# Adding each state's product to the sum with a transfer of its own, in a selective scan between two feed-forward blocks

## The reference

```python
x = x + 0.5 * ffn(layernorm(x), w1, w2, w3)
x = x + attn(layernorm(x), W_x, W_dt, b_dt, A_log, D_param)
x = x + 0.5 * ffn(layernorm(x), w1, w2, w3)

def ffn(x, w1, w2, w3):          # q(w): clip(round(w / mean|w|), -1, 1)
    return (sigmoid(x @ q(w1).T) * (x @ q(w2).T)) @ q(w3).T      # 512 -> 1408 -> 512

def attn(x, ...):                # per token t, channel d, state n
    dt_raw, b, c = split(x @ W_x.T, [128, 16, 16])
    dt = softplus(dt_raw @ W_dt.T + b_dt)
    h = exp(dt * a) * h + dt * b * x       # a = -exp(A_log), a scan over the tokens
    y = sum over n of h * c
    return y + x * D_param
```

## Time and profile before

| | us |
|---|---|
| median of 3 runs | 840.51 |
| lowest, highest | 837.66, 843.51 |
| the profiled execution | 838.59 |
| its span, first to last instruction | 836.7 |
| mean granted PE clock, share of full | 0.894 |

### The profile page before, as it was taken

The page is one execution under the profiler, slowest core; times in us unless marked ns, Lnnn a source line. Parts: engine busy times, 40 slices in busy tenths (PEclk is TensorE's granted clock), DMA queues, the critical chain, the costliest instruction groups (busy, mean ns, idle before and its releaser), DMA issues.

```text
span 836.7 us, 13876 instructions
## 1 busy us (share of the span) xinstructions
PE 651.4 (78%) x4920; PEld 538.5 (64%) x4920; DVE 674.6 (81%) x1079; ACT 554.6 (66%) x1157; POOL 658.4 (79%) x516
## 2 busy tenths in 40 slices
PE   4688587368889888989899888988898876147578
PEld 4576375257677776777578767876687755136367
DVE  4962798699978997899978997899789978799721
ACT  5752764967696678776885679566966795366231
POOL 0261597799899989999899989998999898689112
PEclk7798797679999999999999998999999999569779
DMA  9400378677774978297829784878659673957300
GB/s 362 133 1 1 104 168 180 156 148 163 177 169 108 208 179 187 48 231 167 189 51 227 166 179 111 182 171 173 157 126 202 151 179 82 235 122 141 76 1 26
DMA packets 42694, 122.12 MB, mean 146 GB/s; under 512 B 5888, under 2 KB 14848, under 8 KB 42624
## 3 DMA queue, kind: packets, MB, share of 16 engines
q0 software_dynamic: 19152, 69.74, 44.5%
q1 hardware_dynamic: 23472, 51.49, 18.0%
HBM read 47.03 MB, written 4.46 MB: 62 GB/s over the span
## 4 chain that ended last, share of the span: by engine, by line
POOL 27%; DVE 20%; ACT 17%; PE 15%; issue 14%; DMA 7%; DVEq 0%; POOLq 0%; ACTq 0%
DVE states L881 11%; POOL shared L1078 11%; PE work L392 10%; DMA shared<-shared 7%; POOL hid_lo L1064 6%; PE stat L392 4%; DVE shared L893 3%; POOL shared L1090 3%; ACT decay L700 3%; POOL shared L1089 2%; POOL x_lo L1058 2%; POOL shared L282 1%; ACT tanh L643 1%; ACT hid_hi L651 1%; POOL square L286 1%
## 5 line engine op out<-in xcount | busy, mean ns | idle before, releaser
L1078 POOL TENSOR_TENSOR shared<-shared,b_row 128x1024 f32<-128x1024 f32 x128 | 331.2, 2658 | 39.8 <-DVE shared L282 21.8
L392 PE MATMUL work<-x_hi,q 128*128 128x256 f16 x1408 | 325.8, 281 | 45.8 <-DVE hid L856 25.8
L392 PE MATMUL work<-x_lo,q 128*128 128x256 f16 x1408 | 324.8, 280 | 0.0
L881 DVE TENSOR_TENSOR_SCAN states<-decay,last_state,shared 128x256 f32<-128x256 f32 x448 | 301.7, 738 | 4.9 <-DVE shared L893 0.5
L700 ACT ACTIVATE decay<-shared,a_neg 128x256 f32<-128x256 f32 x512 | 221.9, 468 | 95.6 <-DVE states L881 93.5
L1064 POOL TENSOR_TENSOR hid_lo<-hid,hid_hi 128x256 f16<-128x256 f32 x176 | 144.5, 1102 | 58.0 <-ACT hid_hi L651 57.9
L392 PEld LDWEIGHTS work<-x_hi,q 128*128 128x128 f16 x1408 | 142.5, 101 | 71.6 <-DVE hid L856 30.0
L392 PE MATMUL work<-hid_hi,q 128*128 128x256 f16 x704 | 165.9, 282 | 5.2 <-POOL hid_lo L1064 3.6
L392 PE MATMUL work<-hid_lo,q 128*128 128x256 f16 x704 | 165.9, 282 | 0.0
L893 DVE TENSOR_TENSOR shared<-states,c_row 128x1024 f32<-128x1024 f32 x128 | 156.0, 1219 | 9.5 <-DMA shared<-shared 2.2
L392 PEld LDWEIGHTS work<-x_lo,q 128*128 128x128 f16 x1408 | 141.7, 101 | 22.0 <-issue 1.1
(11 more groups left out here) (99 smaller groups left out, 733.1 us busy)
## 6 DMA issues: line engine op xcount, KB each, us to landing
shared<-shared POOLq DMA_DIRECT2D x133, 512.0 KB, 6.6
b_row<-bc_dram SPq DMA_DIRECT2D x32, 512.0 KB, 4.9
c_row<-bc_dram SPq DMA_DIRECT2D x32, 512.0 KB, 5.2
x_in<-xT SPq DMA_DIRECT2D x8, 512.0 KB, 5.4
outT<-shared SPq DMA_DIRECT2D x7, 512.0 KB, 4.5
shared<-w1T SPq DMA_DIRECT2D x4, 704.0 KB, 6.9
shared<-w2T SPq DMA_DIRECT2D x4, 704.0 KB, 11.8
shared<-w3T SPq DMA_DIRECT2D x3, 768.0 KB, 13.4
```

The lines of the kernel that those rows point to most:

```text
L392: return nc.tensor.matmul(out, lhsT, rhs, start=start, stop=stop)
L881: nc.vector.tensor_tensor_scan(out=states[:, k, :], data0=decay[pair][:, k % 2, :], data1=dbx[:, g % DBX_RING, k, :], initial=state, op0=A ...
L1078: nc.gpsimd.tensor_tensor(dbx[:, g % DBX_RING, :, :], u[:, par, :, :], bcast(b_row[:, group % 2, n % ROWS, :]), ALU.mult).then_inc(dbx_don ...
```

## The change

Each product gets a transfer of its own, issued in the state after it; even states still go to `x2`, odd ones to `y`, and each waits only for the one before it to the same sum. The ring has four single buffers, so a product waits for the transfer of the product four before. `add_y` waits for both last products. There are four semaphores (even and odd products, even and odd chunks) instead of two.

The tables have entries of their own for the first and the last chunk, and the middle order changes too. The softplus on ACT is cut into four pieces with places of their own, as is reading z and reading b and c. `ffn1_due` is general enough to place an entry of FFN 1 beyond a chunk's end; with these tables none lies there. In the middle chunks, on ACT the second identity and the logarithm move behind two gates, the high halves go later, `d_xln` and the high half of layer norm 0 now stand in front of the next chunk's first decays. On DVE the hidden blocks 3 and 4 of FFN 2 go behind the product of state 12, together with `centre` 0; on POOL the low halves 3 to 10 of FFN 2 come after `softplus[2]` and the fold of layer norm 0, and that norm's low half before the product of the next chunk's state 0. The order of PE stays, but for one or two hidden blocks of FFN 2 that move across z and mean 0. In the last chunk `add_y` moves from state 3 to state 1, `centre` 2 one state forward, hidden block 10 of FFN 2 from state 13 to 12, and both residuals into states 14 and 15; in the first, `hidden`, `residual` and the rest of FFN 1 move forward by up to a state, and the middle of layer norm 0 back.

```diff
-DBX_RING, PAIR_RING, X_RING, Y_RING = 3, 2, 3, 2
+DBX_RING, PROD_RING, X_RING, Y_RING = 3, 4, 3, 2
...
 AT_ACT = dict(
-    d_xln=152, dt_raw=101, gate1=[0, 2, 10, 11, 20, 21, 30, 32, 32, 32, 41],
-    gate2=[80, 90, 91, 92, 111, 120, 120, 122, 130, 131, 132], hi1=[2, 11, 20, 21, 22, 31, 32, 41, 41, 41, 42],
-    hi2=[100, 100, 100, 120, 130, 130, 130, 131, 140, 140, 140], logs=120, square0=121, square1=72, square2=50,
-    std0=140, std1=82, std2=60, x_hi0=150, x_hi2=62, z0=110, z1=120)
+    bc_read=101, bc_read_first=100, d_xln=142, d_xln_first=152, dt_raw=101, dt_raw_first=100,
+    gate1=[0, 2, 10, 12, 20, 22, 22, 32, 32, 41, 41], gate1_first=[0, 0, 2, 2, 2, 20, 20, 21, 22, 32, 40],
+    gate2=[72, 82, 91, 100, 112, 112, 120, 121, 131, 131, 132],
+    gate2_last=[80, 81, 91, 92, 92, 92, 101, 111, 111, 112, 121],
+    hi1=[12, 12, 22, 40, 40, 40, 40, 40, 41, 42, 42], hi1_first=[0, 2, 21, 21, 30, 30, 31, 40, 40, 40, 40],
+    hi2=[82, 100, 102, 122, 122, 131, 131, 140, 140, 140, 140],
+    hi2_last=[90, 92, 100, 101, 110, 111, 111, 111, 121, 122, 130], logs=[112, 112, 120, 120],
+    logs_first=[112, 121, 130, 130], square0=130, square0_first=130, square1=80, square1_first=72, square2=50,
+    square2_last=40, std0=140, std0_first=150, std1=90, std1_first=81, std2=60, std2_last=42, x_hi0=150,
+    x_hi0_first=150, x_hi2=61, x_hi2_last=70, z_read=[110, 110, 112, 112], z_read_first=[102, 102, 111, 111])
 AT_DVE = dict(
-    centre0=122, centre1=73, centre2=50, hid1=[2, 10, 12, 13, 22, 23, 32, 40, 42, 42, 43],
-    hid2=[90, 92, 93, 112, 120, 122, 122, 131, 133, 133, 140], norm0=142, norm1=92, norm2=63, recip0=140,
-    recip1=91, recip2=62, res1=[62, 71], res2=[153, 153])
+    centre0=130, centre0_first=132, centre1=73, centre1_first=72, centre2=50, centre2_last=33,
+    hid1=[2, 10, 12, 13, 22, 23, 32, 40, 42, 43, 43], hid1_first=[0, 2, 10, 11, 12, 20, 22, 30, 32, 33, 33],
+    hid2=[81, 83, 103, 123, 123, 130, 130, 131, 132, 140, 141],
+    hid2_last=[81, 90, 93, 93, 102, 103, 112, 113, 121, 122, 123], norm0=143, norm0_first=151, norm1=92,
+    norm1_first=91, norm2=70, norm2_last=62, recip0=141, recip0_first=151, recip1=91, recip1_first=83, recip2=62,
+    recip2_last=60, res1=[61, 71], res1_first=[60, 70], res2=[153, 153], res2_last=[150, 151])
 AT_POOL = dict(
-    add_y=30, fold_sq0=131, fold_sq2=50, lo1=[21, 30, 30, 30, 40, 40, 41, 42, 42, 42, 42],
-    lo2=[112, 112, 112, 131, 132, 132, 132, 132, 132, 132, 132], softplus=[131, 131, 132, 140], x_lo0=150,
-    x_lo2=70)
+    add_y=30, add_y_last=12, fold_sq0=131, fold_sq0_first=132, fold_sq2=50, fold_sq2_last=31,
+    lo1=[21, 22, 32, 42, 42, 42, 42, 42, 42, 42, 42], lo1_first=[20, 20, 30, 31, 31, 31, 31, 31, 31, 32, 32],
+    lo2=[102, 121, 122, 131, 131, 131, 131, 131, 131, 131, 131],
+    lo2_last=[92, 110, 110, 112, 122, 130, 130, 130, 130, 130, 130], softplus=[131, 131, 131, 132],
+    softplus_first=[132, 132, 140, 140], x_lo0=140, x_lo0_first=141, x_lo2=70, x_lo2_last=61)
+
+
+def at(table, c, name):
+    own = name + ("_first" if c == 0 else "_last" if c == NC - 1 else "")
+    return table[own] if own in table else table[name]
...
-            return 32 * (PAIRS * (c // 2) + n)
+        def added(c, n):
+
+            return (odd_added if n % 2 else even_added)[c % 2], 16 * (NS // 2 * (c // 2) + n // 2 + 1)
 
         def prod_of(c, n):
-            return prod[:, 2 * ((NS * c + n) // 2 % PAIR_RING) + n % 2, :, :]
+            return prod[:, (NS * c + n) % PROD_RING, :, :]
...
-                if g // 2 >= PAIR_RING:
-                    before = g // 2 - PAIR_RING
-                    dve.wait_ge(pair_added[before // PAIRS % 2], pairs_added(before // PAIRS, before % PAIRS + 1))
+                if g >= PROD_RING:
+                    dve.wait_ge(*added((g - PROD_RING) // NS, (g - PROD_RING) % NS))
...
-            def add_pair(c, pair):
-
-                if pair == 0:
+            def add_prod(c, n):
+
+                if n == 0:
                     pool.wait_ge(down_read, 2 * ffn1_pass(c) + 2)
+                elif n == 1:
                     pool.wait_ge(d_xln_done, c + 1)
                 else:
-                    pool.wait_ge(pair_added[c % 2], pairs_added(c, pair))
-                pool.wait_ge(prod_done, NS * c + 2 * pair + 2)
-                nc.gpsimd.dma_start(x2(c), prod_of(c, 2 * pair), accum_op=ALU.add).then_inc(pair_added[c % 2], 16)
-                nc.gpsimd.dma_start(y(c), prod_of(c, 2 * pair + 1), accum_op=ALU.add).then_inc(pair_added[c % 2], 16)
+                    pool.wait_ge(*added(c, n - 2))
+                pool.wait_ge(prod_done, NS * c + n + 1)
+                total = y(c) if n % 2 else x2(c)
+                nc.gpsimd.dma_start(total, prod_of(c, n), accum_op=ALU.add).then_inc(added(c, n)[0], 16)
...
                     if s == 0 and not first(c):
-                        add_pair(c - 1, PAIRS - 1)
-                    elif s > 0 and s % 2 == 0:
-                        add_pair(c, s // 2 - 1)
+                        add_prod(c - 1, NS - 1)
+                    elif s > 0 and not (last(c) and s == NS - 1):
+                        add_prod(c, s - 1)
```

194 lines of the change are left out of this document (99 added, 95 removed).

## The result

| | us |
|---|---|
| kernel before, median of 4 runs on the same chip | 839.09 (836.74 to 843.51) |
| changed kernel, median of 4 runs | 852.55 (848.63 to 855.06) |
| ratio, 95% interval | 1.0157 (1.0118 to 1.0196) |
| profiled execution of the changed kernel, its span | 848.63, 846.8 |

The changed kernel is 1.6% slower, where I predicted 1.5% faster. The profiled execution of the changed kernel is the fastest of its four, its span 10.1 us longer than that of before (836.7).

The account below looks back on a forecast made before the run. A middle chunk was taken as a VectorE part, then a ScalarE-then-TensorE part in series. Terms -2.2 -4.7 -3.2 -1.9 +0.5 +0.6 -0.9 -1.2 sum to -13.0 us, from 840.5 to 827.5; range 817 to 840 (own 821 to 832).

Parts of the forecast that it names:

- The low half ahead of the next chunk's first product: POOL, chunk's end: that product ends at about U+30.0 instead of +26.5, DVE wants it at +31.5; costed at nothing.
- y's transfer: Middle chunks: y lands earlier, so DVE's wait at the centring of layer norm 2 goes, -4.7 us over six chunks.
- Ring waits: DVE's waits for product buffers that a transfer hasn't freed go, -2.2 us.
- The last chunk: Earlier y cuts the centring wait (-3.2 us), the down projection wait before the residual goes (-1.9), last products wait (+0.5).
- The middle order, U to residual: Middle chunks, state 11's scans to second residual: square root and second down projection end as before, 0 us.
- The last middle chunk: It has no layer norm 0, so the high halves come sooner there, -0.9 us.
- before U: Middle chunks: gate and high half ahead of a square root cost a hidden-unit slot, +0.6 us over six chunks.
- First chunk: Split softplus lets decays in between, but other waits appear on DVE; -1.2 us (0 to -4).
- Slower: the eight low halves: Rival, chance 0.13: POOL's low halves wait for ACT's late square, delaying six chunks; up to +23 us, 850.
- The slow stretch goes: Rival, chance 0.15: PE's lower-clock stretch in the down projection goes, -10 us more, 817.
- The middle gives nothing: Rival, chance 0.25: middle and first chunks gain nothing; only the last chunk and the -0.9 before it remain, -7.4 us, 833.1.

Follow-up runs that it names:

- e5: Changed kernel with layer norm 0's low half on POOL back behind the next chunk's first product and its transfer: 837.0 us, ratio 0.9988 to the kernel before.
- e8: Kernel before with single transfers, the new first- and last-chunk orders and, in middle chunks, only POOL's order new: 834.2 us, ratio 0.9963.
- e9: As e8, but layer norm 0's low half back behind the next chunk's first product on POOL: 835.6 us, ratio 0.9949 to the kernel before.
- e11: As e5, but each product's transfer halved, leaving half of the products out of the sum: 830.7 us, ratio 0.9896 to the kernel before.
- e1: Kernel before with one transfer for each product and a ring of four, every order as before: 838.1 us, ratio 0.9985.
- e16: As e8, but the last chunk in its old order: 836.7 us, ratio 0.9966 to the kernel before.
- e18: As e5, but ACT's gate of FFN 2 unit 5 behind the logarithm: 835.5 us, ratio 0.9948 to the kernel before.
- e3: Changed kernel with middle chunks in the old order, keeping single transfers and the new first- and last-chunk orders: 838.2 us, ratio 0.9991.

## Why the prediction was wrong, step by step

**The low half ahead of the next chunk's first product: "costed at nothing with 1.5 us of cover left".** This step failed, and it made the kernel slower: with it undone (e5) the changed kernel is level with before, 0.9988. The 13 us that I had promised are missing there too, for the reasons further down. Its place was sized well: the product ends at U+30.7 (U is the end of the scans of state 11; predicted 30.0), and DVE does not wait for it. But I asked only who waits for the product. Behind it on POOL stand the transfers of products 13 to 15 and of the next chunk's first two, then y's, then FFN 1's low halves. In three of the five chunks the transfers moved 0.6 to 2.7 us against e5's, and e5 prices that at 15.6 us (14.2 by the ratios) where the sum has 0. I had also missed the 0.73 us wait for ACT's high half in front of it. Why the same place costs nothing beside the other engines' old orders (e8, e9) is argued above, not shown.

**y's transfer: -4.7.** The mechanism was read wrongly, and the wait that was to go (4.7 us) doubled, to 9.5. I took the landing of 6.6 us as what a transfer takes when one other is ahead, and "lands about 6.6 us after issue" came from counting those ahead. The median of all 133 is 6.6 before and 6.9 after, and from y's issue to the mean it takes 8 to 10 in the middle chunks of both kernels, in a stretch in which the engines' share is 0.97 and more. And not one but two transfers are still under way when y goes out, as before: the products' transfers ahead of it now go out some 3 to 4.6 us apart, and each takes 6 to 10 us there. y took 0.8 us less to land on the mean, not three. And it went out 2.1 us later, counted from U, where I had allowed 0.6; in e5, without the low half in front, it is 0.6. In e11, with half of the bytes, what I had promised is there: no centring wait in any middle chunk. The Trainium skill (DMA: Bandwidth & Descriptors, Anatomy of one DMA) gives 2.0 us and bytes over 436 GB/s. For 256 KB less that is 0.6 us, an estimate; here the medians fell by 2.3 us (6.9 to 4.6). All of the products' transfers were halved there, so a transfer also had fewer bytes of others beside it: the page's figure per transfer doesn't carry over to transfers that add, in a full queue.

**Ring waits: -2.2.** Right: gone in e1 and in the changed kernel. What I didn't price is the transfer that they put ahead of the low halves with the old middle order, 0.8 us a chunk in e1.

**The last chunk: -3.2 for the centring, -1.9 for the residual, +0.5.** The residual's wait is gone and the last sum waits 0.85, inside my 0 to 2. The centring's wait grew from 3.99 to 5.10, against 0.8 predicted. The chunk from product to product fell by 1.1 us, where my terms say 4.6. By e16 its own order is worth nothing that can be measured. What failed in the term of 3.2 is the time of y's issue, which I put at +8 from its place in POOL's order, though `add_y` waits for product 15: it went out at +11.6. Its landing took 6.2 us, about the 6.6 that I had put.

**The middle order, U to residual: 0.** The back part is 0.8 us longer in three of five chunks, 1.2 in one and 0.7 shorter in one; in the one PE's clock fell for longer, in the other not at all. The square root ends at +19.4 and not +18.7 in four of the five, because I laid ACT's gates out by their durations alone and not by when PE has their block ready (0.88 us in the trace; e18 bears it out in part). The low halves end at +22.3 in the same four, instead of +21.6. DVE's stall came out at 2.39 in four chunks, predicted about 3.

**The last middle chunk: -0.9, and before U: +0.6.** The first is right: its back went from 31.9 to 31.0. The second can't be read apart from the fronts' other waits.

**First chunk: -1.2.** The part up to the first middle residual gained 1.4.

**The rivals.** "Slower: the eight low halves" named the right engine, and the sign, but the wrong instruction: they ended 0.5 us later than before, under the 2.2 from which it would decide. "The slow stretch goes" happened only in one chunk of the changed kernel. "The middle gives nothing" came nearest to what the transfers by themselves did, but its 7.4 us from the last chunk weren't there either.

## What to carry to other kernels

When an instruction moves on an engine that also issues transfers, look past the first thing that waits for it: every transfer queued behind it moves too, and where the transfers' share is near 1 a shift of 1 to 3 us can come back larger and unsteady. Before an earlier place is priced, read what the instruction itself waits for: y's transfer couldn't leave before product 15 had landed. Read the share of the transfers in the stretch in which the awaited one is sent (0.97 here), not its mean over a stage (0.73), before its landing time is taken from another place. And an order that has been made for several engines together can't be judged, or taken over, one engine at a time.

## What the runs showed of the hardware

**Adding transfers use more of the engines than plain ones.** The queues of the kernel before, with packets, MB and share of 16 engines' span; the first holds POOL's adding transfers, the second the loads and stores of SyncE:

```profile
q0 software_dynamic: 19152, 69.74, 44.5%
q1 hardware_dynamic: 23472, 51.49, 18.0%
```

69.74 MB in 44.5% of 836.7 us is 187 GB/s while busy; 51.49 MB in 18.0% is 342. Whether it is the adding, or source and destination both being on the chip, or what runs beside them, no run here tells.

**The fall of PE's clock in the down projection is not settled by the idle time ahead of it.** Two stretches of 12 us of e8, each right behind an idle time of 1.97 us (the third number from the end is the granted clock):

```profile
428.50:440.50 12.00, 11.98 (x109) 10.68 (x110) 11.43 (x18) 8.24 (x17) 12.00 (x10) 1.00 0.30 59
518.00:530.00 12.00, 11.64 (x91) 9.78 (x92) 10.00 (x16) 8.58 (x18) 12.00 (x11) 0.86 0.27 51
```

In the first, PE had been idle 1.97 us, as long as before each of the falls of before, and there was none: the back took 32.5 us instead of 34.2. In one chunk of another run (e3) 26 matmuls in place of 15 ran at 0.42 us, with a granted clock of 0.72 over 12 us, and the residual waited 4.10 us:

```profile
350.88 0.69 DVE L894 SCALAR_TENSOR_TENSOR shared<-work,shared 128x512 f32<-128x512 f32 x1 [4.10 <-PE work L424]
```

e3's backs range from 34.4 to 36.3 us, where e1 with the same middle orders has 35.0 each time. So between these chunks the back moves by -1.7 to +1.3 us, with the clock as the difference that the traces show. The Trainium skill (TensorE: Matmul & The Clock Gate, What's actually happening) says that idling brings the throttle back; here the same idle time did so in one chunk and not in another, and what decides it stays open.
